# Two one-column scratch tensors of a fused block become one two-column tensor

## The reference, cut to what matters

```
x = x + layernorm(attn(layernorm(x)))       # x: 16 x 256 x 128, float32
x = x + layernorm(ffn(layernorm(x)))
attn(x): n = ln(x)*g + b
         W1, W2 = mlp_h1(n), mlp_h2(n)      # 128 -> 512 -> 128, gelu between
         t = ln(gelu(tril(W1 @ W2.T) @ n))
         out = x + mlp_fm(ln(x + t))        # 128 -> 512 -> 128
ffn(x):  h = silu(x @ w1.T) * (x @ w2.T)    # 128 -> 512
         h = gelu(h @ h1.T); h = gelu(h @ h2.T)   # 512 -> 512, twice
         out = h @ w3.T                     # 512 -> 128
```

## Time and profile before

| | |
|---|---|
| median of 3 runs | 364.95 us (364.90 to 365.11) |
| profiled execution | 365.25 us |
| its span, first to last instruction | 363.5 us |
| mean granted TensorE clock | 0.995 |
| PE, DVE, ACT, POOL busy, share of the span | 97%, 88%, 83%, 42% |
| instructions | 6043 |

### The profile page before, as it was taken

The page is one execution under the profiler, slowest core; times in us unless marked ns, Lnnn a source line. Parts: engine busy times, 40 slices in busy tenths (PEclk is TensorE's granted clock), DMA queues, the critical chain, the costliest instruction groups (busy, mean ns, idle before and its releaser), DMA issues.

```text
span 363.5 us, 6043 instructions
## 1 busy us (share of the span) xinstructions
PE 351.9 (97%) x1786; PEld 290.1 (80%) x1786; DVE 319.9 (88%) x953; ACT 302.2 (83%) x546; POOL 153.2 (42%) x227
## 2 busy tenths in 40 slices
PE   6999999999999999999999999999999999999991
PEld 5886888788888888888888888888788878778990
DVE  5989999999999999899968999998878998958844
ACT  5999999996888979976789798889698489769890
POOL 3587868430581165109430276025450292053311
PEclk9999999999999999999999999999999999999998
DMA  7614300000000000000000000001010001000101
GB/s 231 174 58 148 114 4 1 0 3 0 3 0 0 2 9 23 0 0 2 1 29 3 0 2 2 0 0 32 1 31 0 0 2 31 0 2 0 32 30 32
DMA packets 8946, 9.08 MB, mean 25 GB/s; under 512 B 720, under 2 KB 6864, under 8 KB 8912
## 3 DMA queue, kind: packets, MB, share of 16 engines
q1 hardware_dynamic: 8368, 8.41, 7.7%
q10 hardware_dynamic: 544, 0.26, 0.3%
HBM read 6.57 MB, written 2.10 MB: 24 GB/s over the span
## 4 chain that ended last, share of the span: by engine, by line
PE 78%; ACT 10%; DVE 6%; issue 2%; DMA 1%; SPq 0%; POOLq 0%; POOL 0%; DVEq 0%; ACTq 0%
PE bank L1236 10%; PE bank L1234 10%; PE bank L1250 8%; PE bank L1251 8%; PE bank L1111 4%; PE bank L1115 4%; PE bank L1112 4%; PE bank L1130 4%; PE bank L1127 4%; PE bank L1128 4%; PE bank L1216 4%; PE bank L1219 4%; PE bank L1055 3%; ACT h_hidden_hi L511 3%; ACT bank L516 2%
## 5 line engine op out<-in xcount | busy, mean ns | idle before, releaser
L722 DVE TENSOR_TENSOR ffn_gate_lo<-bank,ffn_gate_hi 128x512 fp32r<-128x512 f32 (+1 forms) x72 | 43.9, 623 | 8.8 <-ACT bank L587 7.9
L511 ACT ACTIVATE h_hidden_hi<-bank,cols 128x512 fp32r<-128x512 f32 x64 | 43.7, 697 | 7.7 <-PE bank L1115 7.0
L587 ACT ACTIVATE bank<-bank,cols 128x512 f32<-128x512 f32 (+1 forms) x72 | 44.1, 640 | 0.7
L722 DVE TENSOR_TENSOR h_hidden_lo<-bank,h_hidden_hi 128x512 fp32r<-128x512 f32 x64 | 42.3, 677 | 0.4 <-ACT bank L516 0.2
L516 ACT ACTIVATE bank<-bank,cols 128x512 f32<-128x512 f32 x64 | 41.9, 670 | 0.3
L1234 PE MATMUL bank<-ffn_gate_hi,ffn_w_hi 128*128 128x512 f32 (+1 forms) x108 | 40.4, 379 | 0.0
L1236 PE MATMUL bank<-ffn_gate_lo,ffn_w_hi 128*128 128x512 f32 (+1 forms) x108 | 39.6, 373 | 0.0
L581 ACT ACTIVATE ffn_h_hi<-bank,cols 128x512 fp32r<-128x512 f32 (+1 forms) x36 | 23.2, 647 | 13.2 <-PE bank L1236 9.5
L369 POOL TENSOR_TENSOR XR<-X,ln_x_r 128x512 f32<-128x512 f32 x8 | 8.3, 1041 | 52.5 <-DVE bank L867 51.3
L581 ACT ACTIVATE ffn_gate_hi<-bank,cols 128x512 fp32r<-128x512 f32 (+1 forms) x36 | 23.7, 679 | 7.2 <-PE bank L1236 4.3
L1216 PE MATMUL bank<-yT_hi,ffn_w_hi 128*128 128x512 f32 (+1 forms) x72 | 27.0, 379 | 0.2 <-ACT raw L604 0.2
(11 more groups left out here) (162 smaller groups left out, 1118.9 us busy)
## 6 DMA issues: line engine op xcount, KB each, us to landing
raw<-ffn_w SPq DMA_DIRECT2D x5, 512.0 KB, 3.6
out<-X SPq DMA_DIRECT2D x7, 256.0 KB, 2.3
raw<-attn_w SPq DMA_DIRECT2D x6, 256.0 KB, 4.9
X<-x SPq DMA_DIRECT2D x3, 256.0 KB, 5.1
raw<-ffn_w SPq DMA_DIRECT2D x1, 256.0 KB, 3.1
X<-x SPq DMA_DIRECT2D x1, 128.0 KB, 2.4
X<-x ACTq DMA_DIRECT2D x1, 128.0 KB, 2.7
out<-X SPq DMA_DIRECT2D x1, 128.0 KB, 1.9
```

What stands on the lines that cost most here:

```text
L511: nc.scalar.activation(dst, bank(f"{L}u{j}", c)[:, :], ACT.Gelu, bias=bias_of(L, j)).then_inc(*hi[L].done(c, j))
L587: nc.scalar.activation(u, u, ACT.Gelu, scale=cols[:, C_HS[L] + j:C_HS[L] + j + 1]).then_inc(*act2[L].done(c, j))
L722: return nc.vector.tensor_tensor(dst, whole, high.bitcast(f32), ALU.subtract)
```

## The change

The two scratch tensors of one column are declared as one tensor of two columns, and the names `warm` and `quiet` become its columns. The instructions that write them are the same ones, with the same engines, shapes and waits.

```
-        warm, quiet = sb("warm", [P, 1]), sb("quiet", [P, 1])
+        warm_quiet = sb("warm_quiet", [P, 2])
+        warm, quiet = warm_quiet[:, 0:1], warm_quiet[:, 1:2]
```

## The result

The changed kernel takes 361.32 us in the median of four runs (361.23 to 361.65), the kernel before, measured beside it, 364.96 us: a ratio of 0.9901, with a 95% interval of 0.9884 to 0.9919. The forecast was no change.

What follows compares the result with a forecast made beforehand. PE's matmul spacing was taken to bound the kernel; span 363.5 plus 1.75 around it plus 0 for the change gave 365.25 us profiled, 365.0 us for the median, with an 8-in-10 range of 356.5 to 367.0 us.

Steps and rivals of the forecast that it cites:

- What bounds the kernel: PE sets the pace from 84 to 350 us, busy 265.83 of 266; from 20 to 84 DVE and ACT are full too.
- Instructions, and reads and writes of DVE, ACT and POOL: No instruction added, removed or reordered, and the new addresses leave these engines' reads and writes alike; each taken as 0.
- The moving operand: Stream of PE's matmuls, moved from phase 32 to 0 mod 64: taken as 0, at best 20.4 us of gain.
- The proportion argument: Spacings of 233.3 and 116.7 ns for 512 and 256 columns mean cost per column, leaving 0.1 ns per instruction.
- The faster rival, phase of the stream: Each 64-byte piece of PE's stream pays for its phase; half a cycle less saves 6.8 us, giving 358.2 us; chance 0.22.
- The slower rival, weights and stream collide: PE's weight load and stream, now both at phase 0, cost 3.3 ns a matmul: 4.5 us, giving 369.5 us; chance 0.10.
- The chances: For the whole kernel's time: faster 0.40, within 0.2% 0.50, slower 0.10.
- the range: For the whole kernel's time, 8 in 10: 356.5 to 367.0 us.
- the likeliest case: Nothing changes in the kernel's time, 365.0 us; chance 0.50.

Runs made afterwards that it cites:

- The second experiment: The changed kernel with 32 bytes of unused space behind the merged scratch tensor, so working tensors return to their old addresses; 365.07 us, ratio 0.9992.
- the bare measurement: Block left out, PE alone running groups of matmuls with chosen starts of weights and stream; 512 columns took 226.7 ns at distance 0, 233.3 at 32.
- experiments 4 and 9: 4: changed kernel, weights moved to phase 32, distance 96, 365.50 us. 9: kernel before, weights and streams both at 160 mod 256, distance 0, 361.50 us.
- (16,16): Group with PE alone, weights and stream both starting at 16 bytes, distance 0, float32r, 512 columns; 230.0 ns a matmul.
- (0,0): Group with PE alone, weights and stream both starting at 0 bytes, float32r; 226.7 ns a matmul for 512 columns, 120.0 for 256.

## Why the prediction was wrong, point by point

*What bounds the kernel:* right. PE's spacing is the one number that moved, and PE's lead at its end is 3.45 us, where the medians differ by 3.64.

*Instructions, and reads and writes of DVE, ACT and POOL:* right, all 0. The second experiment takes the merge by itself and finds nothing.

*The moving operand, "I take 0":* this is the step that failed. The effect was real: with the stream's start moved by 32 bytes against the weights, the spacing went from 233.3 to 227.5 ns, which is the gain. The trace of before had no row for 512 columns at another address, and I took the weight loads' duration at both phases for the nearest one. That row measures how long a load takes; what changed is the spacing of pairs of load and stream, and no duration of either shows it: a load still takes 188 ns and a matmul of 512 columns still 0.39 us.

*The proportion argument:* wrong. I held that 233.3 against 116.7 ns leaves nothing for a cost per matmul. At distance 0 the two are 226.7 and 120.0, and in the bare measurement distance 64 gives 229.2 and 117.8 and distance 32 itself 233.3 and 118.0. That they were 2 to 1 in the kernel before is therefore no sign of a cost per column alone.

*The faster rival, phase of the stream, 0.22:* right in sign and in the size of a steady matmul (6.7 ns foretold, 6.6 between the bare groups, 5.8 in the rows shown), wrong in the cause, which experiments 4 and 9 refute from both sides. It priced the total at 6.8 us; 3.6 came. Three things took the rest.

First, settling. Behind each break, such as transposes or scores, PE takes some spacings to find the rhythm of 227 ns. In the 33 unbroken runs of 12 or more matmuls in the changed kernel, the first nine average 230.2 ns and the later ones 227.2; in the kernel before it is 232.8 and 233.3. Over all uninterrupted spacings below 241 ns, worked out from the starts, the mean is 228.5 against 233.0, so 4.5 ns a matmul and not 6.6.

Second, where 256 columns run unbroken they lose about 3 ns each (116.8 to 119.7 in the last chunk), where this rival had them gain 3.3. In the lead this is small: it shrinks by 0.16 us over the last chunk.

Third, waits. From 84 to 326 us of the kernel before, 867 wide matmuls have an undisturbed spacing; 4.5 ns each is 3.9 us, but the lead grows by 3.17 us over them. The disturbed ones (spacing over 245 ns) went from 49 with 15.1 us to 55 with 17.3 us. Most of these are no waits: 48 stand at the same places in both kernels, nearly all at the first matmul behind transposes or scores, with some 280 to 320 ns in either. Seven are new, one is gone, and these with two that grew cost PE 0.78 us, which is the difference. The longest stand at 216.64 us, where 0.48 us pass before a transpose of `raw` that POOL wrote (0.23 in the kernel before), and at 318.99, where 0.54 us pass before the matmul of `ffn_h_lo` that DVE wrote (0.40 before).

So a faster PE meets a few operands that aren't ready, with DVE now busy for 89% of that stretch (233.74 of 262.5 us); for six of these ten places the trace names no engine that PE waited for. Before 84 us PE gains still less: the lead there is 0.44 us, where 252 matmuls at 4 to 6 ns would give 1.0 to 1.5. The forecast let none of PE's gain through there, as DVE and ACT are full; about a third came through.

*The slower rival, weights and stream collide:* it was right that the two addresses together decide, and its sign was wrong; whether the two reads collide stays open. Its evidence was two rows of 256 columns at 120 ns with both operands alike, and 120.0 is just what 256 columns came to in the changed kernel. The error was to carry that over to 512 columns, where the same distance is among the best and not the worst. It was also set up for phases mod 64; the period is 256.

*The chances:* faster had 0.40, and the time fell within the range, but the likeliest case was given as no change. That the range held is luck: its lower end was drawn for a gain of 6.8 us from another cause.

What stays open: why the distance matters, and why by 256 bytes. That PE's two reads hinder each other in SBUF is a guess that fits most of it; no run tells it from, say, the order in which PE fetches its operands, and it doesn't explain why (16,16) is slower than (0,0), or why 256 columns are slowest where 512 are fastest. Nor was it tried whether the settling can be avoided.

The Trainium skill says in SBUF — State Buffer, Who interferes with whom, that PE has two read ports to SBUF, one for the stream and one for weight loads, which are independent, and that PE never waits on anyone. For the other engines the runs agree: PE alone shows the same 226.7 and 233.3 ns as in the full kernel. That the two ports are independent of each other is not borne out for float32r, where the spacing goes from 226.7 to 236.7 ns by the relation of the two addresses alone. For bfloat16 the Trainium skill, in TensorE: Matmul & The Clock Gate, Back-to-back issue gap, gives some 216 ns for an isolated matmul of 512 columns and some 131 ns for a sustained stream of loads and matmuls; the groups here are such a stream, and they took 216, so the first figure is the one that fits.

## What to carry to other kernels

Where PE is the bound and its matmuls are float32r of 512 columns, read the spacing of an unbroken run at the full granted clock first. If it is 233 ns and not 227, lay out SBUF so that weights and moving operands start at the same remainder mod 256, both at a multiple of 32; one unused tensor of the right size is enough. A steady matmul gains 2.8% by it (233.3 to 226.7 ns), and this kernel gained 1.0% in all. Matmuls of 256 columns get some 3 ns slower by the same layout. Then pad whatever is declared ahead of them so that later edits of small tensors don't shift it, and when a change that adds or drops a small tensor moves the time, compare the addresses before anything else. An absent row isn't filled by its neighbour: where two things run at once, the duration of each says little about the spacing of the pair.

## What the runs showed that was not expected

The spacing of float32r matmuls depends on the distance from weights to stream down to single columns (226.7 ns at 0 and 240 bytes, 236.7 at 4), repeats by 256 bytes where that was tried (distances 0 and 32), and for 256 columns orders the distances differently than for 512 (120.0 ns at 0, 118.0 at 32). A stream can have two steady rhythms at one and the same distance (233.2 and 226.7 ns at 240), so that a bare measurement with one history can promise what a kernel doesn't get.
